# A new order of keys, score groups, outputs, turned maxima and projection within a step of attention

## What is computed

```python
x = x + 0.5 * ffn(layernorm(x))
x = x + attn(layernorm(x))
x = x + 0.5 * ffn(layernorm(x))
# attn
q, k, v = heads(einsum('bsh,oh->bso', x, w_qkv))
scores = einsum('bhqd,bhkd->bhqk', q, k) / sqrt(16)
scores = where(causal, scores, finfo.min)
attn = einsum('bhqk,bhkd->bhqd', softmax(scores), v)
return einsum('bsh,oh->bso', merged(attn), w_o)
```

## Time and profile before

| | us |
|---|---|
| median of 3 runs | 826.29 (824.8 to 826.83) |
| the profiled execution | 823.37 |
| its span, first to last instruction | 821.6 |
| PE busy in the span | 766.5 |
| DVE, ACT, POOL busy | 434.2, 376.2, 316.8 |
| mean granted clock of TensorE | 0.96 of full |

### The profile page before, as it was taken

How to read it: one execution, slowest core, us unless ns; L and a number is a source line. 1 busy time by engine, 2 the same in 40 slices (tenths; PEclk the granted TensorE clock), 3 DMA queues, 4 the chain that set the end, 5 groups by cost and what they waited for, 6 DMA issues and landing times. The chain is left out here.

```text
span 821.6 us, 16019 instructions
## 1 busy us (share of the span) xinstructions
PE 766.5 (93%) x6176; PEld 675.1 (82%) x6176; DVE 434.2 (53%) x850; ACT 376.2 (46%) x630; POOL 316.8 (39%) x373
## 2 busy tenths in 40 slices
PE   9689999999999987898998989967899999999997
PEld 5579999999999975565665655655899999999997
DVE  5945445534634226767676675456446345444630
ACT  4415545634544301556646556513345445544631
POOL 6073454464424263232232122222644554463133
PEclk9779999999999997899999999986999999999999
DMA  9542553354242154201222010024541553454122
GB/s 305 160 147 74 146 141 93 87 155 126 47 121 27 16 166 154 76 18 72 78 81 106 33 70 11 26 78 126 182 128 41 155 134 82 107 146 117 26 27 25
DMA packets 61862, 80.27 MB, mean 98 GB/s; under 512 B 10916, under 2 KB 48804, under 8 KB 61812
## 3 DMA queue, kind: packets, MB, share of 16 engines
q1 hardware_dynamic: 46452, 60.34, 21.8%
q0 software_dynamic: 15360, 19.23, 12.8%
HBM read 49.62 MB, written 19.01 MB: 84 GB/s over the span
## 5 line engine op out<-in xcount | busy, mean ns | idle before, releaser
L655 DVE SCALAR_TENSOR_TENSOR second_h_lo<-second_ps_h,second_h_hi 128x320 fp32r<-128x320 f32 x128 | 63.0, 492 | 105.2 <-ACT second_h_hi L514 105.2
L655 DVE SCALAR_TENSOR_TENSOR first_h_lo<-first_ps_h,first_h_hi 128x320 fp32r<-128x320 f32 x128 | 62.9, 492 | 104.8 <-ACT first_h_hi L514 104.8
L418 POOL DMA_INDIRECT after_first<-first_scaled,first_add_now x40 | 69.4, 1736 | 117.5 <-ACT first_scaled L507 110.9
L418 POOL DMA_INDIRECT out_dram<-second_scaled,second_add_now x40 | 69.0, 1725 | 117.2 <-ACT second_scaled L507 111.5
L1180 DVE TENSOR_REDUCE at_maxima<-at_ps_front 128x4 f32<-128x512 f32 (+2 forms) x96 | 97.0, 1040 | 21.1 <-PE at_ps_front L1321 20.6
L1052 POOL TENSOR_SCALAR_AFFINE_SELECT at_probs<-at_probs 128x512 f32<-128x512 f32 x64 | 41.3, 658 | 147.0 <-ACT at_probs L1110 147.0
L776 PE MATMUL second_ps_o<-second_w_hi,second_h_hi 128*128 128x256 f32 x320 | 90.9, 284 | 0.0
L776 PE MATMUL first_ps_o<-first_w_hi,first_h_hi 128*128 128x256 f32 x320 | 90.7, 283 | 0.0
L776 PE MATMUL second_ps_o<-second_w_lo,second_h_hi 128*128 128x256 f32 x320 | 89.7, 280 | 0.0
L776 PE MATMUL second_ps_o<-second_w_hi,second_h_lo 128*128 128x256 f32 x320 | 89.7, 280 | 0.0
L776 PE MATMUL first_ps_o<-first_w_lo,first_h_hi 128*128 128x256 f32 x320 | 89.5, 280 | 0.0
(11 more groups left out here) (297 smaller groups left out, 1763.5 us busy)
## 6 DMA issues: line engine op xcount, KB each, us to landing
first_w_raw<-in_L_ffn_w_dram SPq DMA_DIRECT2D x16, 1024.0 KB, 8.9
second_w_raw<-in_L_ffn_w_dram SPq DMA_DIRECT2D x15, 1024.0 KB, 5.7
at_q_stack<-at_pre_hi SPq DMA_DIRECT2D x12, 256.0 KB, 2.5
at_k_stack<-at_pre_hi SPq DMA_DIRECT2D x12, 256.0 KB, 2.6
x<-_attn_hidden_states_dram SPq DMA_DIRECT2D x4, 512.0 KB, 5.4
after_first<-x SPq DMA_DIRECT2D x4, 512.0 KB, 7.8
normed_rows<-first_xn SPq DMA_DIRECT2D x4, 512.0 KB, 4.6
x<-after_first SPq DMA_DIRECT2D x4, 512.0 KB, 5.6
```

Source lines behind the costliest of these rows:

```text
L418: pool.indirect_dma_start(sum_rows, bass.IndirectOffsetOnAxis(ap=add_now[par][:, s:s + 1], axis=0), scaled[par][:, s, :], None, bounds_che ...
L655: v.scalar_tensor_tensor(h_lo[:, f, a * HALF:(a + 1) * HALF], ps_h[:, f % 2, a, 0:HALF], 0.0, h_hi[:, f, a * HALF:(a + 1) * HALF].bitcast( ...
```

## The change

One return statement of `step_plan`, the one for ordinary steps (v = -1 to 13). `S` are the six score groups, `N` the six keys.

```diff
         if v == UNITS - 1:
             return N[0] + [("logits", 1)] + N[1] + N[2] + [("turn_x", 2)] + N[3] + outputs + N[4] + [("logits", 2)] + N[5]
-        return (N[0] + S[0] + S[1] + N[1] + S[2] + N[2] + S[3] + N[3] + normal + turns + N[4] + S[4] + project +
-                outputs + S[5] + work + N[5])
+        return (outputs + N[0] + S[0] + S[1] + N[1] + S[2] + N[2] + normal + N[3] + S[3] + N[4] + S[4] + turns +
+                N[5] + work + S[5] + project)
```

## The result

The changed kernel takes 832.05 us (median of 20 runs, 824.88 to 836.17); the kernel before, timed beside it, 825.37 (median of 20). The ratio is 1.0084, with a 95% interval of 1.0063 to 1.0104: slower by 0.8%. Predicted were 833.7 us, with 827 to 840 as the range. The sign, the range and nearly the size held. The way to it did not, as the rows show: the size is right by luck.

A forecast was written before the change was run, and what follows sets the result against it. PE, busy 93%, sets the pace, with a small toll from DVE. New waits of 24.3 us less old 17.1 give +7.2; +0.5 and -0.3 make +7.4, so profiled 823.37 becomes 830.8, the median 833.7; range 827 to 840.

The forecast's parts named there:

- The plain step: A step without special items waits 1.36 us at N3, turns and work, where step 9 waited 1.14; eight make 10.9.
- the chain of maxima: DVE's reductions of S0 to S4, one behind another; the work starts 6.23 us after the value matmuls end.
- the gap that I saw at N3: N3 needs N1's exponential on ACT, so it starts at 2.98 us and S3 is complete only at 3.99.
- the bound for a chain without gaps: If DVE ran without any gap from 0.89 on, the work would start at 5.7: +0.4 us in all, 826.7.
- The steps that turn finished heads: Steps 4, 8, 10, 12: four transposes, some 0.5 us, sit in the wait, which shrinks to 0.95; 3.8 in all.
- rival 2: A wash: DVE's reductions run without gaps, a step's new waits about as long as its old ones; 826.7 us, chance 0.13.
- rival 3: The clock falls more often: gaps at step 14 and in steps 2 and 6, three falls add 4.2 us, 838; chance 0.13.
- normalize: Its 2.02 us of statistics on DVE move S3's reduction by 1.73; steps 2 and 6 wait 3.1 and 2.7 us.
- The landing: Arrival of the turned maxima's transfer after step 13: N0 of step 14 waits 2.3 us (0.9 to 2.7).
- project: At the end of step 7, PE waits for copies and the last subtraction of rows: 1.4 us (0 to 2).
- Step -1: Its turns stands nearer to the next step's N0: +0.5 us (0 to 1).
- The signs that I named: PE's waits on maxima grow, those on low halves nearly vanish, steps 2 and 6 exceed 14 us, step 14 waits about 2.

## Why the prediction was right, and where it wasn't

The time was right by luck: two terms were missed, by about as much and in opposite directions.

**The plain step: wrong, by 0.45 us a step.** Forecast: 12.52 - 1.14 + 1.36 = 12.74. Measured: 12.29. The step of the prediction that failed is the chain of maxima, and in it the start of S1. I took S0's 0.62 us on PE (458.62 to 459.24 of the earlier trace rows) as PE's own time; in the changed kernel S0 takes 453.13 - 452.80 = 0.33. In the kernel before, ACT was copying the values out of the slot that S1 wants until 458.16 + 1.02 = 459.18, by its timeline:

```profile
458.16 1.02 ACT L1092 ACTIVATE at_v_ones<-at_ps_front 128x1024 f32<-128x1024 f32 x1 [3.00 <-PE at_ps_front L1266]
```

S1 starts 0.06 after that. It was a wait that no list of waits shows, and the new order removes it, since S5, T and PV now lie between the work and S1. (With outputs first in the old order S0 takes 0.32.) S1's 0.70 up to N1 was too long in the same way: it takes 453.60 - 453.13 = 0.47; what it waited for, the rows don't settle. So N1 comes 1.14 after N0 and not 1.60, the gap that I saw at N3 doesn't open, and the maxima run in one piece: the work starts 5.82 after N0, where I had 6.23, and 5.7 as the bound for a chain without gaps. The steps that turn finished heads are as long (12.32 for steps 4 and 10): as forecast, their transposes lie in the wait. So the bound was the case, and by it the sum is +0.4 and not +7.4: rival 2 had the mechanism of the plain step.

**The clock: wrong, by what rival 3 was about.** I gave it a chance of 0.13 and priced it at 1.4 us a fall, three falls, from the earlier trace rows. All three falls came, at the three places named, and they cost 9.1 us together, 4.2 by my price. The price was taken from one fall, and without its end: 438 to 440 still has 0.86 of the clock, so that fall lasted 3.4 us and cost about 1.7 (an estimate from the granted clock of the three windows). The fall of step 2 is as long and cost 1.6; those of step 6 and step 14 last two and four times as long and cost 2.6 and 6.1. The Trainium skill (TensorE: Matmul & The Clock Gate, HAM oscillation), which tells that idle gaps between groups of matmuls lower the clock, agrees with the trace at each of the three.

**The sum again.** The chain without gaps gives +0.4. The kernel before has two falls of its own between 336 and 536, which the one with matmuls in the gaps doesn't have in its profiled execution: 1.7 us for the one of the earlier trace rows, and for 510 to 514 some 4 x (1 - 0.57) = 1.7, both estimates from the granted clock. That is 0.4 - 3.4 = -3.0 without any fall, and -2.7 was measured with matmuls in the gaps. The 9.1 us of the clock make it +6.1; measured are +6.7. The +7.4 of the prediction is near that because two errors nearly cancel: 7.0 too much for the chain of maxima, and 9.1 - 3.4 = 5.7 for the clock, which the sum put at nothing.

**normalize: right as a wait.** I expected waits 1.75 and 1.35 longer than a plain step's; without the clock the two steps are 1.7 and 2.0 longer than the 12.29 of one. That they take over 14 us held. Step 6 was put lower than step 2 and was not; in the changed kernel it is also the one where the clock is at half already when turns starts.

**The landing: right.** N0 of step 14 waits 2.01 us; expected 2.3 (0.9 to 2.7). The two issues of the transfer start at 504.42 and take 1.29 together, so the second starts at about 505.06 and its data are used 1.96 later; I had taken 2.05. The Trainium skill (DMA: Bandwidth & Descriptors, Latency and other measured facts) gives about 2 us as the fixed cost of a DMA; the 1.96 agree with it. **project** in step 7: 1.1 measured, 1.4 expected. **Step -1**: N0 of step 0 waits 0.9, I had 0.5 (0 to 1). **POOL's clears** behind normalize cost nothing, as expected: no wait for them is listed.

**The signs that I named.** Waits before turns and the work, the low halves gone, 14 us in steps 2 and 6, and 2 us ahead of step 14 are all there. That PE's waits on maxima grow is not: 3.1 us are listed where 8.5 were. With the 6.6 before turns they make 9.7, but 4.2 of that are the gaps of steps 2 and 6, so that the other steps have 5.5. By my own sign (wrong if they shrink) I was wrong on the plain step. That I would be wrong if a plain step took 12 us or less held only by 0.3, and was the wrong test: it should have been the 12.52 of before.

## What to carry to other kernels

Price a reordering by what each engine does *behind* a gap as well as in it: here three gaps of 2 us cost some 6 us as waits and 9 as half clock, and moving the two items that make them (normalize behind the last keys, one turns forward) turned a loss of 0.8% into a gain of 0.8%. Before a duration between two starts is taken as an engine's own time, look at what the other engines do to the buffer that the second one writes: a start that follows 0.06 us after another engine's end is a wait, listed or not. And put long statistics on the engine that paces a chain of small reductions only where that chain is done.

## What the runs showed of the hardware

The size of the clock's toll was not expected. A gap of 2.12 us in a PE that was busy 93% of its time was followed by a fall of the granted clock from 1.00 to 0.50, in step 2 and in step 6, for 3.4 and 6.8 us; at the gap of 2.01 ahead of step 14, behind which transposes and waits followed, it stayed for 13.7. Seventeen matmuls without a use in each gap kept it at 1.00 from 336 to 536. A gap isn't needed for a fall: the kernel before has one at 510 with PE listed as busy in all of the 4 us ahead. The half clock also shows as *busy* time: PE's busy sum rose by 9.3 us with the same 6176 instructions, so a longer busy time of PE is a sign to look at its clock.

The gaps do not cost the same in every execution. Two of the 20 of the changed kernel, with a mean granted clock of 0.959 and 0.961, took 825.25 and 824.88 us, as the kernel before; two with 0.939 took 836.09 and 836.17. What decides that wasn't found.
